# Four edits to the order of work around the layer norms of a two-layer graph network

## The chip, the cores and the metric

One core of one Trainium2 chip runs the whole program. The metric is device time in microseconds (us) of one execution, from the inputs in HBM to the output in HBM. Several executions are timed; their median counts.

## The reference

x is 128 graphs of 128 nodes with 256 features, adj a 0/1 matrix per graph. All is float32.

```python
h = maximum(layernorm(x), 0)
x = x + L0(h, adj)       # scores = leaky_relu(h W a1 + (h W a2)^T), masked by adj, softmax; elu(attn @ h)
h = maximum(layernorm(x), 0)
x = x + L1(h, adj)       # three attention blocks:
# for l in 0..2:
#   scores = si + sj^T + attn_b[l], leaky 0.2, mask = adj + eye, softmax
#   agg = attn @ x ;  h = layernorm(x + agg) * g1 + beta1
#   ff  = gelu(h @ W1[l] + b1[l]) @ W2[l] + b2[l]
#   x   = layernorm(h + ff) * g2 + beta2
```

W1 is 256 x 1024, W2 1024 x 256. Every matmul of the feed-forward part is made of three: each operand is split into a high part that the fast format holds and a low part that is the rest, and high x high, high x low and low x high are added.

## The kernel before

**Units, groups, steps.** Four graphs are a group (32 groups), and a group in one of the three blocks of L1 is a unit (96 units, run in chunks of 8 groups: 8 units of layer 0, 8 of layer 1, 8 of layer 2, then the next chunk). Every engine runs the same list of steps, `body`, from step -6 to step 97. Step s does the feed-forward part of unit s on PE (`hidden(0..7)`: eight blocks of 128 hidden features; `second(0..3)`: the four graphs), and beside it, on the other engines, the norm ahead of it for unit s + 1, the softmax for unit s + 2, the dots for unit s + 3 and the norm behind it for unit s - 1. Steps 24 to 47 are a loop that is run twice; 72 to 97 are written out.

**Stages of L0.** Each group passes through L0 in four stages, one step after another: early (norm of the input, dots, mask), middle (scores, exponentials), late (aggregation, ELU, residual), end (norm of the result). The first eight groups do so from step -6 on, one in every step. From step 2 on a group starts in every third step. So from step 5 to 73 three kinds of step take turns:
- an **opening step** (5, 8, 11, ... 71) has the early stage of one group and the end stage of another,
- a **mask step** (6, 9, ...) has a middle stage,
- an **ELU step** (7, 10, ...) has a late stage.

Three in this order are called a triple here. Step 74 has the last end stage; steps 75 to 94 have no stage of L0: **bare steps**. Steps 0 to 4 still end one of the first eight groups each and run another order of DVE's work.

**Engines.** PE multiplies. ACT evaluates: for each hidden block the Gelu twice (L872 writes the high half g_hi, L874 the exact value back into the PSUM bank), exponentials (L739), the products of the norms (L746, L801), and `turned` (L843), which copies the turned exponentials into et. DVE makes the low halves (`g_low(c)`, L1000: exact value minus high half), the sums and statistics, the shifts of the norms (L990) and the dots (L969, `row_dots`). POOL makes the inverse roots (L1310, `inverse_root`), products and additions of rows (`by_graph`, L374) and the masks (L1374, L1365). SP issues the DMAs. Each engine works through its own list in order; counted semaphores tie them.

**PE in a step** (L687 on): hidden(0), the scores of unit s + 2 (`next_scores`, L556), which wait for the dots of that unit and for et_ready, since et is read out of the same bank; the aggregates of unit s + 1 (L569), which read et; hidden(1) to hidden(7); the turned rows; second(0) to second(3). hidden(1) writes into a bank that DVE must have emptied first (`v_done`, L1207: vb, the first graph pair). second(0) reads low half c before its block c.

**DVE in a step, from 5 on** (L1245 to L1280): vb, half 0, the sums of the rows of unit s + 1, half 1, its variance, the lows, half 2, its norm, half 3, the statistics of the input (early stage), halves 4 and 5, the statistics of vb (`second_statistics`), half 6, the variance of vb (`second_variance`), half 7, the variance of the input, the low rows, the shifts of both, then

```python
next_dots(range(T // 2))
made_variance(); next_inverses(); made_shift()
if not only_middle(s): first_lows()
next_dots(range(T // 2, T))
elu_sums(); first_inverses(); first_dots(); next_heads(); first_heads()
```

next_dots are the eight dots of unit s + 3, first_dots the eight of the early stage's group; made_variance and made_shift belong to the end stage, and POOL's root (`made_root`) lies between the two. ACT's `make_rows` (L746) waits for made_shift, and `turned` stands behind make_rows in ACT's list.

**POOL in a step**: root of the norm of unit s + 1, the rows hb (eight instructions), the root of unit s - 1, the roots of the stages, the masks, residual_sum (late stage), weight halves in the first chunk (L1326), then, behind a wait for all dots of the step, `affine` of unit s - 1: xo times g2, plus beta2; for a unit of the last layer `residual` adds the kept rows xin[1] besides. The twelve instructions of that are L374 too. ACT writes xo before (L746), and SP stores it after.

**The start.** DVE awaits the constants aw_in at the beginning of step -3. In step -1 ACT runs: exponentials, make_rows, ELUs, first exponentials, turned.

## Time and profile before

| | us |
|---|---|
| runs shown | 2748.73, 2750.09, 2750.27 |
| median | 2750.09 |
| the profiled execution | 2747.82 |
| its span | 2746.0 |
| PE busy | 2657.8 |
| ACT busy | 2200.4 |
| DVE busy | 2136.6 |
| POOL busy | 1676.9 |

The span runs from the first to the last instruction; 1.8 us of the profiled execution lie around it. PE's mean granted clock is 0.988 of 2.4 GHz: it is at half speed, 1.2 GHz, in parts of the first 128 us only. A matmul is pipelined, so PE's gaps between one matmul's modelled end and the next one's start tell more than its busy share. A releaser ("<-") is what ended an idle time; where an engine waits for several semaphores the last one is named.

### The profile page before, as it was taken

How to read it: one execution, taken by the hardware profiler on the slowest of the kernel's cores; microseconds unless marked ns; L12 is line 12 of the kernel's file. 1: busy time of each engine (PE TensorE's matmuls, PEld its weight loads, DVE VectorE, ACT ScalarE, POOL GpSimd, SP SyncE). 2: the span in 40 equal slices, each digit the busy share in tenths (PEclk: the TensorE clock that was granted, in tenths of full speed). 3: DMA queues.
4: the chain of work that ended last, by engine and by line, in shares of the span. 5: the costliest groups of instructions: out<-in, count | busy, mean ns of one | idle time of the engine just before them, and what ended most of it. 6: DMA issues, size and time to landing. Idle time of an engine off the chain costs nothing.

```text
span 2746.0 us, 53334 instructions
## 1 busy us (share of the span) xinstructions
PE 2657.8 (97%) x16772; PEld 2394.5 (87%) x16868; DVE 2136.6 (78%) x7999; ACT 2200.4 (80%) x4494; POOL 1676.9 (61%) x2181
## 2 busy tenths in 40 slices
PE   5799999999999999999999999999999999999997
PEld 4689888988888888988888989898888898998997
DVE  7998788877787877787877787877788767677674
ACT  5899888888788888887888888888888777777774
POOL 4567657656666656566666566556676554454555
PEclk7899999999999999999999999999999999999999
DMA  6222222222222222112322121222132211111121
GB/s 217 79 70 72 92 73 88 67 77 87 81 76 69 75 67 71 62 64 82 100 82 80 50 77 66 78 66 80 62 103 82 68 36 53 47 41 53 51 64 54
DMA packets 118589, 203.43 MB, mean 74 GB/s; under 512 B 12800, under 2 KB 85536, under 8 KB 118304
## 3 DMA queue, kind: packets, MB, share of 16 engines
q1 hardware_dynamic: 118304, 199.97, 22.4%
q8 instruction: 137, 2.24, 0.3%
q14 instruction: 148, 1.21, 0.1%
HBM read 116.05 MB, written 83.89 MB: 73 GB/s over the span
## 4 chain that ended last, share of the span: by engine, by line
PE 72%; DVE 11%; POOL 8%; issue 5%; ACT 3%; DMA 0%; SPq 0%; DVEq 0%; POOLq 0%; ACTq 0%
PE bank L610 32%; PE bank L593 27%; PE ps_u L569 7%; POOL xo L374 3%; DVE g_lo L1000 3%; DVE st L974 2%; PE ps_u L651 2%; POOL rs L1310 2%; POOL hb L374 2%; PE ps_s L564 2%; DVE ub L1093 2%; PE ps_s L556 2%; DVE ub L969 1%; ACT g_hi L872 1%; ACT bank L874 1%
## 5 line engine op out<-in xcount | busy, mean ns | idle before, releaser
L610 PE MATMUL bank<-w_hi,g_hi 128*128 128x256 f32 x3072 | 892.0, 290 | 15.4 <-DVE g_lo L1000 15.2
L610 PE MATMUL bank<-w_hi,g_lo 128*128 128x256 f32 x3072 | 866.8, 282 | 0.0
L610 PE MATMUL bank<-w_lo,g_hi 128*128 128x256 f32 x3072 | 865.6, 282 | 0.0
L872 ACT ACTIVATE g_hi<-bank,b_eff 128x512 fp32r<-128x512 f32 x768 | 529.3, 689 | 334.0 <-PE bank L593 327.3
L1000 DVE TENSOR_TENSOR g_lo<-bank,g_hi 128x512 fp32r<-128x512 f32 x768 | 519.0, 686 | 202.6 <-ACT bank L874 187.9
L593 PE MATMUL bank<-zt_hi,w_hi 128*128 128x512 f32 x1536 | 633.2, 412 | 9.1 <-DVE g_lo L1000 5.5
L593 PE MATMUL bank<-zt_hi,w_lo 128*128 128x512 f32 x1536 | 608.3, 396 | 0.0
L593 PE MATMUL bank<-zt_lo,w_hi 128*128 128x512 f32 x1536 | 607.1, 395 | 0.0
L610 PEld LDWEIGHTS bank<-w_hi,g_hi 128*128 128x128 f32 x3072 | 579.9, 189 | 24.1 <-DVE g_lo L1000 23.1
L610 PEld LDWEIGHTS bank<-w_lo,g_hi 128*128 128x128 f32 x3072 | 580.2, 189 | 0.7
L610 PEld LDWEIGHTS bank<-w_hi,g_lo 128*128 128x128 f32 x3072 | 579.6, 189 | 0.0
L1310 POOL TENSOR_TENSOR rs<-ve,neg_half 128x4 f32<-128x4 f32 x256 | 266.6, 1041 | 445.6 <-DVE ve L985 441.0
L874 ACT ACTIVATE bank<-bank,b_eff 128x512 f32<-128x512 f32 x768 | 508.4, 662 | 25.0
L374 POOL TENSOR_TENSOR xo<-xo,g_row 128x256 f32<-128x256 f32 x380 | 268.8, 739 | 201.4 <-ACT xo L746 136.5
L374 POOL TENSOR_TENSOR hb<-ub,g_row 128x256 f32<-128x256 f32 x384 | 272.4, 741 | 173.3 <-DVE ub L1093 168.2
L593 PEld LDWEIGHTS bank<-zt_hi,w_hi 128*128 128x128 f32 x1536 | 290.1, 189 | 75.7 <-DVE g_lo L1000 10.8
L593 PEld LDWEIGHTS bank<-zt_hi,w_lo 128*128 128x128 f32 x1536 | 289.6, 189 | 67.6
L593 PEld LDWEIGHTS bank<-zt_lo,w_hi 128*128 128x128 f32 x1536 | 290.4, 189 | 60.0
L1207 DVE TENSOR_TENSOR vb<-bank,hb 128x512 f32<-128x512 f32 x192 | 129.9, 688 | 242.9 <-PE bank L610 214.6
L374 POOL TENSOR_TENSOR hb<-hb,bb_row 128x256 f32<-128x256 f32 x384 | 277.8, 756 | 7.5
L969 DVE CUSTOM_DVE_ANT_0 ub<-xb,aw_row 128x256 f32<-128x256 f32 x744 | 280.5, 432 | 1.6 <-issue 0.5
L374 POOL TENSOR_TENSOR xo<-xo,beta_row 128x256 f32<-128x256 f32 x380 | 267.5, 736 | 7.5
(96 smaller groups left out, 4146.1 us busy)
## 6 DMA issues: line engine op xcount, KB each, us to landing
xb<-x_scratch SPq DMA_DIRECT2D x88, 512.0 KB, 4.0
x_scratch<-xo SPq DMA_DIRECT2D x64, 512.0 KB, 4.8
xin<-in_x SPq DMA_DIRECT2D x38, 512.0 KB, 4.8
r_scratch<-elu_r SPq DMA_DIRECT2D x32, 512.0 KB, 3.0
xin<-r_scratch SPq DMA_DIRECT2D x32, 512.0 KB, 4.5
out<-xo SPq DMA_DIRECT2D x32, 512.0 KB, 3.4
m<-m_scratch SPq DMA_DIRECT2D x96, 128.0 KB, 3.9
x_scratch<-h SPq DMA_DIRECT2D x24, 512.0 KB, 2.9
```

What stands on the lines that cost most here:

```text
L374: ins = eng.tensor_tensor(dst[:, t, :], src[:, t, :], other(t), op)
L556: pe.matmul(scores[:, t * P:(t + 1) * P], dot[:, 1, t:t + 1].to_broadcast((P, P)), ident[:, :], is_transpose=True, start=(t == 0), stop=Tr ...
L564: mm = pe.transpose(dst[:, t * P:(t + 1) * P], e[:, t, :], ident[:, :])
L569: pe.matmul(sums[t // 2][:, t % 2 * D:(t % 2 + 1) * D], weights[:, t, :], rows[:, t, :], start=True, stop=True).then_inc(done, 1)
L593: mm = pe.matmul(bank[turn[c]][:, :], w[:, l, k, c * P:(c + 1) * P], z[:, k, :], start=(n == 0), stop=(n == 3 * K1 - 1))
L610: mm = pe.matmul(y, g[:, c, r * P:(r + 1) * P], w[:, l, c, :], start=(c == 0 and n == 0), stop=(c == C - 1 and n == 2))
L872: act.activation(g_hi[:, c, :], block_in, ACT.Gelu, bias=bias).then_inc(g_hi_ready, 1)
L874: act.activation(block_in, block_in, ACT.Gelu, bias=bias).then_inc(gelu_done, 1)
L969: dve.tensor_tensor_reduce(junk[:, j, :], rows[:, t, :], vec(j), 1.0, 0.0, ALU.mult, ALU.add, dot[:, j, t:t + 1]).then_inc(ready, 1)
L1000: dve.tensor_tensor(g_lo[:, c, :], bank[turn[c]][:, :], g_hi[:, c, :].bitcast(F32), ALU.subtract).then_inc(g_lo_ready, 1)
L1207: dve.tensor_tensor(vb[:, 2 * r:2 * r + 2, :], ps_y[r].rearrange("p (t d) -> p t d", d=D), hb[(s - 1) % 2][:, 2 * r:2 * r + 2, :], ALU.add ...
L1310: pool.tensor_tensor(rs[:, :], ve[:, :], neg_half[:, :], ALU.pow).then_inc(rs_ready, 1)
```

## The change

- DVE, steps 5 on: halves 4 to 7 follow each other; the statistics of vb come behind them, then a copy of four columns into `spare` (it stands between statistics and variance, whose wait it takes), then the variance.
- DVE, where a step has an early and an end stage (the opening steps): the order behind made_variance is next_inverses, the first four dots of the early group, made_shift, the last four next_dots, the last four first_dots. first_dots from step 0 on write their products into the other half of the scratch ub and await `h_scaled` and `zt_ps` instead of all next dots.
- POOL, units of the last layer: `residual` adds beta2 onto the kept rows xin[1] in place. It stands behind the masks and ahead of residual_sum, behind a wait for the first four next dots. affine then multiplies xo by g2 and adds xin[1]: eight instructions behind ACT's xo instead of twelve. For the last unit DVE's affine does the same, and the addition onto xin[1] is POOL's.
- ACT, step -1: turned comes ahead of the ELUs and the first exponentials.
- DVE, start: the wait for the constants moves from the beginning of step -3 to just ahead of its next_dots.

```diff
--- before.py
+++ after.py
@@ -254,7 +254,7 @@
         nm2_ready = sem("nm2_ready")
         z2_ready = sem("z2_ready")
         xo_scaled = sem("xo_scaled")
-        xo_shifted = sem("xo_shifted")
+        r_shifted = sem("r_shifted")
         xo_ready = sem("xo_ready")
 
 
@@ -382,14 +382,15 @@
             eng.wait_ge(z2_ready, st.nth(u))
             by_graph(eng, xo, xo, lambda t: g2_row[:, l, :], ALU.mult).then_inc(xo_scaled, 1)
             eng.wait_ge(xo_scaled, st.nth(u))
-            by_graph(eng, xo, xo, lambda t: beta2_row[:, l, :], ALU.add).then_inc(xo_shifted if last else xo_ready, 1)
+            if last:
+                eng.wait_ge(r_shifted, st.nth0(group(u)))
+            by_graph(eng, xo, xo, lambda t: xin[1][:, t, :] if last else beta2_row[:, l, :], ALU.add).then_inc(xo_ready, 1)
 
         def residual(eng, st, u):
 
             if layer(u) == L - 1:
-                eng.wait_ge(xo_shifted, st.nth0(group(u)))
                 eng.wait_ge(r_in, 16 * st.nth0(group(u)))
-                by_graph(eng, xo, xo, lambda t: xin[1][:, t, :], ALU.add).then_inc(xo_ready, 1)
+                by_graph(eng, xin[1], xin[1], lambda t: beta2_row[:, L - 1, :], ALU.add).then_inc(r_shifted, 1)
 
         block = ctx.enter_context(nc.Block())
 
@@ -855,10 +856,14 @@
                     high_rows()
                     if s == -1:
                         next_exps()
+                        make_rows()
+                        turned()
+                        elus()
+                        first_exps()
+                        return
                     make_rows()
                     elus()
-                    if s < -1:
-                        next_exps()
+                    next_exps()
                     first_exps()
                     turned()
                     return
@@ -1034,9 +1039,11 @@
                     if v0 is not None:
                         if s >= 0:
                             dve.wait_ge(h0_ready, st.nth0(v0, T))
-                        if live(s + 3) and s >= 0:
-                            dve.wait_ge(dots_ready, st.nth(s + 3, 2 * T))
-                        row_dots(st.nth0, v0, dots0, h0[v0 % 2], lambda j: v_row[:, j, :], dots0_ready, junk,
+                            if live(s + 1):
+                                dve.wait_ge(h_scaled, st.nth(s + 1))
+                                dve.wait_ge(zt_ps, st.nth(s + 1))
+                        row_dots(st.nth0, v0, dots0, h0[v0 % 2], lambda j: v_row[:, j, :], dots0_ready,
+                                 vb if s < 0 else ub[:, 2:4, :],
                                  graphs, made=h0_ready if s < 0 else None)
 
                 def sum_rows():
@@ -1185,6 +1192,8 @@
                     made_shift()
                     first_dots(range(T // 2, T))
                     low_rows()
+                    if s == -3:
+                        dve.wait_ge(aw_in, 16 * 2)
                     next_dots(range(T))
                     first_heads()
                     next_heads()
@@ -1253,10 +1262,11 @@
                 input_statistics()
                 g_low(4)
                 g_low(5)
+                g_low(6)
+                g_low(7)
                 second_statistics()
-                g_low(6)
+                dve.tensor_copy(spare[:, 2:2 + T], neg_half[:, :])
                 second_variance()
-                g_low(7)
                 input_variance()
                 if v1 is not None and early_step(v1) >= 0:
                     mask_sums(v1)
@@ -1269,22 +1279,27 @@
                 next_dots(range(T // 2))
                 made_variance()
                 next_inverses()
-                made_shift()
-                if not only_middle(s):
-                    first_lows()
-                next_dots(range(T // 2, T))
-                elu_sums()
-                first_inverses()
-                first_dots()
+                if v0 is not None and v3 is not None:
+                    first_dots(range(T // 2))
+                    made_shift()
+                    next_dots(range(T // 2, T))
+                    first_dots(range(T // 2, T))
+                else:
+                    made_shift()
+                    if not only_middle(s):
+                        first_lows()
+                    next_dots(range(T // 2, T))
+                    elu_sums()
+                    first_inverses()
+                    first_dots()
                 next_heads()
                 first_heads()
                 if late_piece(s) is not None:
                     late_low_half(*late_piece(s))
                 if s - 2 == U - 1:
                     affine(dve, st, s - 2)
-                    residual(dve, st, s - 2)
-
-            steps(dve, body, {-3: lambda: dve.wait_ge(aw_in, 16 * 2), -1: rows})
+
+            steps(dve, body, {-1: rows})
 
 
         @block.gpsimd
@@ -1410,6 +1425,10 @@
                     made_root()
                 mask()
                 first_mask()
+                if live(s - 1) and layer(s - 1) == L - 1:
+                    if live(s + 3):
+                        pool.wait_ge(dots_ready, st.nth(s + 3, 2 * T, T))
+                    residual(pool, st, s - 1)
                 residual_sum()
                 if late_piece(s) is not None:
                     late_low_half(*late_piece(s))
@@ -1420,7 +1439,6 @@
                     if v0 is not None:
                         pool.wait_ge(dots0_ready, st.nth0(v0, 2 * T))
                     affine(pool, st, s - 1)
-                    residual(pool, st, s - 1)
 
             steps(pool, body, {})
```

## Rows read from the trace of the kernel before

**Rows 1.** The page, part 1: busy us, share of the span, instructions of each engine.

```profile
PE 2657.8 (97%) x16772; PEld 2394.5 (87%) x16868; DVE 2136.6 (78%) x7999; ACT 2200.4 (80%) x4494; POOL 1676.9 (61%) x2181
```

**Rows 2.** Waits of PE: line, releaser; us in total, times, longest.

```profile
PE bank L610 <- DVE g_lo L1000: 15.2, 29, 1.4
...
PE bank L593 <- issue: 1.6, 1, 1.6
```

**Rows 3.** Sums by stretch: us, busy us (instructions) by engine, PEclk, DMA share, GB/s.

```profile
2472.35:2524.86 52.51, 52.41 (x339) 47.56 (x339) 37.54 (x132) 39.01 (x74) 26.55 (x37) 1.00 0.15 46
...
913.76:940.74 26.98, 26.45 (x170) 23.86 (x170) 23.06 (x90) 22.52 (x45) 17.45 (x22) 1.00 0.29 94
...
940.74:996.08 55.34, 55.23 (x356) 50.10 (x357) 42.35 (x160) 45.88 (x96) 32.20 (x43) 1.00 0.16 56
...
sum 752.66, PE 739.58 PEld 665.03 DVE 593.85 ACT 616.13 POOL 512.94; mean PE 246.53 PEld 221.68 DVE 197.95 ACT 205.38 POOL 170.98
```

**Rows 4.** Timeline of DVE, step 29: start us, us, line, operation, [idle before <-releaser].

```profile
927.90 1.40 DVE L974 BATCH_NORM_STATS2 st<-vb 128x6 f32<-128x256 f32 x4
...
930.58 0.68 DVE L1000 TENSOR_TENSOR g_lo<-bank,g_hi 128x512 fp32r<-128x512 f32 x1
...
933.11 0.43 DVE L969 CUSTOM_DVE_ANT_0 ub<-xb,aw_row 128x256 f32<-128x256 f32 x1
...
934.50 1.40 DVE L974 BATCH_NORM_STATS2 st<-elu_r 128x6 f32<-128x256 f32 x4
...
936.42 0.17 DVE L985 TENSOR_SCALAR ve<-mv 128x4 f32<-128x4 f32 x1
...
937.71 0.16 DVE L990 SCALAR_TENSOR_TENSOR nm<-mv,rs 128x4 f32<-128x4 f32 x1 [1.04 <-POOL rs L1310]
...
938.20 0.82 DVE L969 CUSTOM_DVE_ANT_0 ub<-xb,aw_row 128x256 f32<-128x256 f32 x1
...
938.96 0.41 DVE L969 CUSTOM_DVE_ANT_0 ub<-xb,aw_row 128x256 f32<-128x256 f32 x1
```

**Rows 5.** Timeline of PE, end of step 29 and start of step 30.

```profile
931.31 0.39 PE L610 MATMUL bank<-w_hi,g_hi 128*128 128x256 f32 x1 [0.47 <-DVE g_lo L1000]
...
942.14 0.60 PE L556 MATMUL ps_s<-ident,dots 128*128 128x128 f32 x4
...
944.33 0.58 PE L593 MATMUL bank<-zt_hi,w_hi 128*128 128x512 f32 x1
```

**Rows 6.** Timeline of ACT, step 29.

```profile
928.24 0.66 ACT L874 ACTIVATE bank<-bank,b_eff 128x512 f32<-128x512 f32 x1
...
939.90 0.57 ACT L843 ACTIVATE et<-ps_s 128x512 f32<-128x512 f32 x1
```

**Rows 7.** Timeline of DVE, step 21, a mask step of layer 2.

```profile
703.31 1.38 DVE L1093 TENSOR_SCALAR ub<-ub,mv,rs 128x256 f32<-128x256 f32 x4 [1.52 <-POOL rs L1310]
```

**Rows 8.** Timeline of POOL, step 29.

```profile
930.74 2.09 POOL L1310 TENSOR_TENSOR rs<-ve,neg_half 128x4 f32<-128x4 f32 x2
...
937.91 2.17 POOL L1374 TENSOR_SCALAR m<-adj_i 128x512 bf16<-128x512 int32 x1
```

**Rows 9.** Timelines of PE, ACT and DVE, steps -3 to 0.

```profile
97.11 1.08 PE L556 MATMUL ps_s<-ident,dots 128*128 128x128 f32 x4 [3.43 <-ACT et L843]
...
96.30 0.67 ACT L843 ACTIVATE et<-ps_s 128x512 f32<-128x512 f32 x1
...
104.11 0.69 DVE L1000 TENSOR_TENSOR g_lo<-bank,g_hi 128x512 fp32r<-128x512 f32 x1 [0.54 <-ACT bank L874]
...
39.27 1.41 DVE L974 BATCH_NORM_STATS2 st<-ub 128x6 f32<-128x256 f32 x4 [4.21 <-DMA ab_col<-in_L_gnn_attn_b]
...
41.07 13.65 PE L546 MATMUL bank<-beta_col,raw 128*128 128x1 f32 x64
```

**Rows 10.** Timelines of DVE, step 11, and PE, step 12.

```profile
441.99 0.95 DVE L969 CUSTOM_DVE_ANT_0 ub<-h,v_row 128x256 f32<-128x256 f32 x1
...
447.50 0.50 PE L593 MATMUL bank<-zt_hi,w_hi 128*128 128x512 f32 x1 [0.88 <-DVE vb L1207]
```

## The prediction

> **What bounds the kernel now.** I read the page first, for who is busy: PE for 97% of the span [rows 1]. Next the waits of PE, for what the rest is: beside the first steps, small waits on DVE's low halves, 15.2 us in 29 places [rows 2]. Then the sums by stretch, for the steps they sit in [rows 3]. Two bare steps take 52.51 us, 26.26 each; a mask step with the ELU step behind it takes 55.34, without a gap. So a triple without stalls is 26.26 + 55.34 = 81.60 us. In layers 0 and 1 the opening step is 26.98, 0.72 over the bare one, and that is all such a triple loses. The nine triples that hold the last-layer units (three stretches of three, from 581, 1243 and 1907 us) take 752.66 us: 18.3 above 9 x 81.60, of which 1.6 is PE's own stop where the loop turns [rows 2]. They lose 16.7 us.
>
> The timelines say where. In opening step 29 DVE has half 5 behind it at 927.90, does vb's statistics first (to 929.30), then half 6 and vb's variance, and starts half 7 at 930.58 [rows 4]; PE sits 0.47 us for it [rows 5]. ACT had its input ready at 928.24 + 0.66 = 928.90 [rows 6]. In layer 2 POOL stands in twelve products and additions when the next norm's root is due: DVE waits 1.52 us for it in step 21 [rows 7], and PE behind DVE.
>
> **Low halves in one row.** Half 6 would run at 927.90, half 7 when ACT is done, 928.94 to 929.63. PE needs it at about 930.84 (0.47 before 931.31), so the opening step falls to the bare 26.26: **-0.72**, and PE reaches its next step 0.72 earlier. vb's statistics then end near 930.95 and its variance 0.7 later (as 935.90 to 936.59, the copy included) [rows 4]. POOL's two roots of 2.09 us run from 931.72 to 933.81, against 930.74 to 932.83 [rows 8], and the dots behind the shifts begin at 934.09 instead of 933.11 [rows 4]. In steps of the other kinds the statistics move behind a half that DVE must await, and the low rows come some 1.5 us later. The cover there is PE's work: by the same count the ELU step's aggregates, the nearest taker, keep about 1 us in hand. Without it every ELU step would pay.
>
> **Dots around the root.** From the first dot to the made group's variance is 936.59 - 933.11 = 3.48, so the variance ends at 937.57. Four dots of the new input follow in 1.39 (933.11 to 934.50) [rows 4], and the made group's shift starts at 938.96 instead of 937.71. The 1.04 us of waiting is gone, but what was waited for comes later. POOL begins its mask 937.91 - 936.59 = 1.32 after that variance, at 938.89, 0.07 before the shift. A DVE instruction that came 0.29 us after the mask's start took 0.82 instead of 0.42 [rows 4, 8]. The bounds for the shift are no delay and that 0.40, its end 939.12 or 939.52; I take the second, the nearest row.
>
> ACT goes from that shift to the end of et in 940.47 - 937.87 = 2.60 us [rows 4, 6], and PE's next scores wait for et: where that is seen they start 0.14 us behind its end [rows 9]. So they run at 942.26 (or 941.86). PE would be ready at 942.14 - 0.72 = 941.42 [rows 5]. **New wait: 0.84 (or 0.44)**, ahead of the scores of the mask step. A triple of layer 0 or 1 comes to -0.72 + 0.84 = +0.12 (or -0.28); eleven of them, opened by steps 14 to 62: **+1.3 (or -3.1)**. The dots' new waits on scaled and turned rows hide: the first half of the next dots has awaited both. Their other scratch costs nothing; operands and sizes stay.
>
> **Residual rows in place.** POOL's work stays at twelve products and additions per last-layer unit, but four leave the path behind the norm, so the next root is no longer late: the stall of [rows 7] goes, and the opening step's with it. The four now follow the mask. In an opening step that ends at 938.89 + 2.17 = 941.06 [rows 8]; the residual rows are long there, since SP issues their load right behind the previous unit's store. DVE is then at its last four dots, from 939.52 + 1.39 = 940.91. The nearest row is step 11, where four POOL additions met such dots: 0.95 each instead of 0.42, so 0.88 apart instead of 0.35 [rows 10]. That gives 940.91 + 0.35 + 3 x 0.88 = 943.90; two short heads, which meet POOL's last additions, about 0.8 with them; vb's first half, 0.69, ends near 945.4. In step 12 PE started right behind such a half [rows 10]. PE's second hidden block would want it at 944.33 - 0.72 = 943.61 [rows 5]: **1.8, taken as 1.9, lost in the mask step**, the 0.84 included. Bounds: 0.84 (POOL hits nothing) and 2.3 (both heads hit in full). Eight triples lose 1.9, and the one at the loop's turn, whose 1.6 us covers most, 0.4: 15.6 against 16.7, **-1.1**. In ELU steps the same meeting falls into DVE's own wait for the ELU parts, in mask steps ahead of its wait for PE.
>
> The rule that speaks most against this is in the Trainium skill, SBUF — State Buffer, section "SBUF: two separate sides": the port pair that VectorE and GpSimd share is an exclusive lock, held for a whole instruction. Taken literally it gives the first rival below; here a mask of 2.17 us cost DVE 0.40 [rows 4, 8], so the sum goes by the rows.
>
> **The rest.** Steps 5, 8 and 11 end in weight halves, and vb is already what PE waits for behind them. DVE's stalls there change from 1.04 to 0.35 (half 7), about 0.55 (shifts) and 0.08 (copy): **-0.2** for the three. In step -1 et no longer stands behind ELU and exponentials; PE's scores now wait 3.43 us for it. They would then wait for dots that end at about 94.9, and DVE, dense through step 0, gains its stall of 0.54 at 104.11 [rows 9] and some 0.15 ahead of it: **-0.7** (0 to -2.2). The constants' wait frees 4.21 us of DVE before 39.27, but PE stands in the bias products from 41.07 for 13.65 us either way [rows 9]: **0**. At the end unit 94 leaves POOL some 0.6 earlier, while unit 95's residual now awaits its load on POOL and meets DVE's product: **0** (-0.6 to +0.6).
>
> **Sum:** +1.3 - 1.1 - 0.2 - 0.7 + 0 = -0.7 us. The profiled execution took 2747.82, 2.27 below the median; on the median of 2750.09 that is **2749.4 us**. About 0.2%, 5.5 us, is what a measurement of this kernel can tell. The forecast's own bounds (unmet mask -4.4, heavier heads +3.2, start and end) give 2742 to 2755.
>
> **Rivals.** First, the shift waits for POOL's whole mask. Then it ends at 941.06 + 0.16 = 941.22, the scores run at 943.96, 2.54 late: eleven triples lose 1.82 net, 20.0, and the last-layer ones, with dots and vb also 1.7 later, 3.6 each, 14 more than now; with the rest +33, **2783**. For it: the new shift falls just behind the mask's start. Against it: a dot 1.05 us into a mask took 0.41 [rows 4]. This is the lock of the Trainium skill's page named above; by that rule it would be the result. Chance 0.04. The same in part: the path from et to the scores costs 20 x 0.1 = 2 us for every 0.1 us that the shift ends behind 939.52, and from 0.3 us on (939.8) the change is slower: chance 0.10, around **2757**.
>
> Second, POOL's residual additions don't slow the dots, or the heads absorb it. Then the last-layer triples lose 0.84 each, the loop's none: 6.7 - 16.7 = -10.0, in all **2740**; with the mask unmet too, 3.5 - 16.7 = -13.2 and -3.1, **2733**. For it: a POOL instruction slowed only what came soon behind its start [rows 4]. Against it: step 11, where every dot was hit [rows 10]. Chance 0.27 together, 0.09 of it for the second.
>
> Third, the opening stall is ACT's and not DVE's order: no half comes earlier, et is not exposed, and the time stays within the forecast's range. Half 7's input at 928.90 against its start at 930.58 [rows 4, 6] leaves it 0.02.
>
> **The numbers.** Forecast 0.57; with the third rival no change has 0.59; faster 0.27; slower 0.04 + 0.10 = 0.14. The range leaves out the far rivals of both sides (0.09 and some 0.08): 2738 to 2757.
>
> **What would show it.** Right: opening steps of 26.3 without a wait on low halves; a wait of 0.4 to 0.8 us of PE's scores on ACT's et in some twenty mask steps; in layer 2 dots of 0.95 and a PE wait on vb, and no DVE wait on POOL's root. Wrong: triples of layer 2 near 82.4 us (POOL harmless), or mask steps over 28 in layers 0 and 1 (the shift held by the mask).

## The result, and the profile after

The changed kernel takes 2735.68 us (median of 5 runs, 2735.10 to 2736.28) against 2750.27 for the kernel before on the same chip: ratio 0.9949, interval 0.9938 to 0.9960. It is faster by 14.6 us; no change had been forecast, and the result lies 2.3 us below the range. Its profiled execution has a span of 2734.1 us against 2746.0, so 11.9 us of the gain can be followed in the two traces.

The page, part 1, after [rows 1]:

```profile
PE 2653.5 (97%) x16772; PEld 2385.7 (87%) x16868; DVE 2193.9 (80%) x8088; ACT 2203.1 (81%) x4494; POOL 1703.4 (62%) x2185
```

PE does the same work and is busy 4 us less; DVE is busy 57 us longer and the kernel is faster. The waits of PE after [rows 2]:

```profile
PE bank L594 <- DVE vb L1216: 4.9, 12, 1.8
PE bank L611 <- DVE g_lo L1005: 4.6, 6, 1.4
PE ps_s L557 <- ACT et L844: 4.2, 16, 0.4
PE bank L594 <- issue: 1.6, 1, 1.6
```

The 29 waits for low halves are down to 6, all in the first steps; waits for et (16) and for vb (12) have come instead. The sums by stretch after [rows 3]: two bare steps, opening step 29, the two steps behind it, and the sum of the nine layer-2 triples:

```profile
2460.10:2512.61 52.51, 52.41 (x339) 47.53 (x340) 38.31 (x134) 39.24 (x74) 26.61 (x37) 1.00 0.15 46
907.62:933.88 26.26, 26.21 (x171) 23.79 (x170) 22.74 (x89) 20.61 (x41) 16.47 (x22) 1.00 0.31 96
933.88:989.63 55.75, 55.39 (x355) 49.95 (x356) 43.21 (x164) 47.79 (x100) 33.33 (x44) 1.00 0.16 56
...
sum 746.44, PE 738.25 PEld 661.76 DVE 631.80 ACT 616.07 POOL 529.18; mean PE 246.08 PEld 220.59 DVE 210.60 ACT 205.36 POOL 176.39
```

The opening step has the length of a bare one, the mask step has 0.42 more than before, and the nine layer-2 triples have become 6.2 us shorter.

**Opening step 29 after** [rows 4, 6, 8], timelines of DVE, ACT, POOL and of PE in step 30:

```profile
931.15 0.17 DVE L990 TENSOR_SCALAR ve<-mv 128x4 f32<-128x4 f32 x1
...
931.38 0.43 DVE L974 CUSTOM_DVE_ANT_0 ub<-h,v_row 128x256 f32<-128x256 f32 x1
...
932.77 0.16 DVE L995 SCALAR_TENSOR_TENSOR nm<-mv,rs 128x4 f32<-128x4 f32 x1
...
933.20 0.82 DVE L974 CUSTOM_DVE_ANT_0 ub<-xb,aw_row 128x256 f32<-128x256 f32 x1
```

```profile
934.95 0.58 ACT L844 ACTIVATE et<-ps_s 128x512 f32<-128x512 f32 x1
```

```profile
931.40 1.28 POOL L1325 TENSOR_TENSOR rs<-ve,neg_half 128x4 f32<-128x4 f32 x1 [3.83 <-DVE ve L990]
932.65 0.25 POOL L1320 TENSOR_TENSOR spare<-neg_half 128x1 f32<-128x1 f32 x1
932.97 2.11 POOL L1389 TENSOR_SCALAR m<-adj_i 128x512 bf16<-128x512 int32 x1
```

```profile
935.67 0.62 PE L557 MATMUL ps_s<-ident,dots 128*128 128x128 f32 x4 [0.26 <-ACT et L844]
```

POOL's root takes 1.28 us beside DVE's dots, not the 1.01 it took while DVE stood still, so the mask starts 0.20 behind the shift's start. The root before:

```profile
936.67 1.01 POOL L1310 TENSOR_TENSOR rs<-ve,neg_half 128x4 f32<-128x4 f32 x1 [3.84 <-DVE ve L985]
```

The mask slows one of the last next dots instead (0.82). From the end of the shift to the end of et are 2.60 us, as forecast.

**Opening step 20, layer 2, after**, timelines of DVE, POOL and of PE in step 21:

```profile
684.05 0.17 DVE L990 TENSOR_SCALAR ve<-mv 128x4 f32<-128x4 f32 x1
...
687.46 0.41 DVE L974 CUSTOM_DVE_ANT_0 ub<-h,v_row 128x256 f32<-128x256 f32 x1
...
688.15 0.94 DVE L974 CUSTOM_DVE_ANT_0 ub<-h,v_row 128x256 f32<-128x256 f32 x1
...
689.02 0.93 DVE L974 CUSTOM_DVE_ANT_0 ub<-h,v_row 128x256 f32<-128x256 f32 x1
...
689.88 0.68 DVE L1086 TENSOR_SCALAR si<-dots,ab_col 128x4 f32<-128x4 f32 x1
...
690.55 1.28 DVE L1216 TENSOR_TENSOR vb<-bank,hb 128x512 f32<-128x512 f32 x2
```

```profile
687.96 3.26 POOL L374 TENSOR_TENSOR xin<-xin,beta_row 128x256 f32<-128x256 f32 x4
```

```profile
691.28 0.50 PE L594 MATMUL bank<-zt_hi,w_hi 128*128 128x512 f32 x1 [0.23 <-DVE vb L1216]
```

POOL's additions start half a microsecond behind the last four dots, not 0.15 as worked out. The first two dots escape, two take 0.93 or 0.94 and one head 0.68 instead of the 0.22 that it takes in step 29. vb's first half follows and PE waits for it.

### The profile page after: what moved, and what is told of

Its sections match the earlier page's. It is cut to its first block, busy times and chain, and to the rows that moved or that the text cites. A ratio compares the mean times of both kernels' runs of the same rounds, so it can differ in the third digit from the quotient of the medians.

```text
span 2734.1 us, 53457 instructions
## 1 busy us (share of the span) xinstructions
PE 2653.5 (97%) x16772; PEld 2385.7 (87%) x16868; DVE 2193.9 (80%) x8088; ACT 2203.1 (81%) x4494; POOL 1703.4 (62%) x2185
## 4 chain that ended last, share of the span: by engine, by line
PE 74%; DVE 12%; POOL 6%; ACT 5%; issue 4%; DMA 0%; DVEq 0%; SPq 0%; POOLq 0%; ACTq 0%
PE bank L594 31%; PE bank L611 30%; PE ps_u L570 7%; POOL hb L374 3%; DVE ub L974 3%; PE ps_u L652 2%; DVE st L979 2%; POOL rs L1325 2%; PE ps_s L557 2%; PE ps_s L565 2%; ACT g_hi L877 1%; ACT bank L879 1%; DVE g_lo L1005 1%; DVE ub L1100 1%; ACT h L747 1%
## 5 line engine op out<-in xcount | busy, mean ns | idle before, releaser
L1325 POOL TENSOR_TENSOR rs<-ve,neg_half 128x4 f32<-128x4 f32 x256 | 275.7, 1080 | 554.4 <-DVE ve L990 553.0
L974 DVE CUSTOM_DVE_ANT_0 ub<-xb,aw_row 128x256 f32<-128x256 f32 x744 | 311.2, 475 | 1.4
L374 POOL TENSOR_TENSOR hb<-hb,bb_row 128x256 f32<-128x256 f32 x384 | 272.3, 741 | 7.5
L747 ACT ACTIVATE xo<-vb,nm,rs 128x256 f32<-128x256 f32 x384 | 199.4, 595 | 28.6 <-DVE nm L995 19.7
```

Of the source, the lines that this page charges most:

```text
L374: ins = eng.tensor_tensor(dst[:, t, :], src[:, t, :], other(t), op)
L747: a = act.activation(dst[:, t, :], src[:, t, :], function, bias=nm[:, t:t + 1], scale=rs[:, t:t + 1])
L974: dve.tensor_tensor_reduce(junk[:, j, :], rows[:, t, :], vec(j), 1.0, 0.0, ALU.mult, ALU.add, dot[:, j, t:t + 1]).then_inc(ready, 1)
L1325: pool.tensor_tensor(rs[:, :], ve[:, :], neg_half[:, :], ALU.pow).then_inc(rs_ready, 1)
```

## The experiments

The change has five edits; the table holds all kernels that were timed: medians, and lengths of single steps taken from PE's first hidden matmul to the next step's. Steps 29 and 30 are an opening and a mask step of layers 0 and 1, 44 and 45 of layer 2; 48 follows the loop's turn, 95 runs to the end of the span. "5 at" is when step 5 starts. y1, which is the kernel before profiled once more, stands in the text alone.

| kernel | median | 5 at | 29 | 30 | 44 | 45 | 48 | 95 |
|---|---|---|---|---|---|---|---|---|
| before | 2750.3 | 249.28 | 26.98 | 26.90 | 27.31 | 27.88 | 27.55 | 38.08 |
| changed | 2735.7 | 248.37 | 26.26 | 27.32 | 26.27 | 27.96 | 29.25 | 38.44 |
| x1 rows | 2764.1 | 251.76 | 26.26 | 27.67 | 26.28 | 29.50 | 29.29 | 40.34 |
| x2 dots | 2741.7 | 250.49 | 27.19 | 26.97 | 27.32 | 26.88 | 26.98 | 38.03 |
| x3 residual | 2750.8 | 251.58 | 26.99 | 26.90 | 27.01 | 28.17 | 29.63 | 36.29 |
| x4 constants | 2747.3 | 247.28 | 26.98 | 26.90 | 27.33 | 27.94 | 27.48 | 38.12 |
| y2 et, step -1 | 2750.2 | 250.78 | 26.97 | 26.90 | 27.30 | 27.90 | 27.53 | 38.05 |
| y3 rows, dots | 2743.3 | 251.57 | 26.26 | 27.31 | 26.27 | 28.29 | 28.83 | 40.28 |
| x5 changed, no residual edit | 2740.0 | 249.50 | 26.26 | 27.31 | 26.28 | 28.27 | 28.61 | 40.26 |
| x6 changed, dots as before | 2773.7 | 248.97 | 26.26 | 27.65 | 26.27 | 31.22 | 31.19 | 38.27 |
| z1 changed, no additions | 2728.7 | 249.38 | 26.26 | 27.32 | 26.27 | 27.31 | 28.79 | 35.97 |
| x7 changed, et first | 2731.0 | 247.71 | 26.26 | 26.88 | 26.27 | 27.97 | 30.62 | 38.14 |
| x8 = x5, et first | 2735.9 | 251.15 | 26.26 | 26.88 | 26.27 | 28.28 | 28.74 | 40.27 |
| y4 = x7, residual in the gap | 2727.1 | 248.48 | 26.26 | 26.88 | 26.27 | 27.54 | 29.19 | 38.11 |
| z2 = y4, next dots first | 2726.8 | 248.11 | 26.26 | 26.88 | 26.27 | 27.54 | 28.75 | 38.35 |

### One edit at a time, on the kernel before

**x1**, halves 4 to 7 in one row, alone:

```diff
                 g_low(5)
-                second_statistics()
                 g_low(6)
-                second_variance()
                 g_low(7)
+                second_statistics()
+                dve.tensor_copy(spare[:, 2:2 + T], neg_half[:, :])
+                second_variance()
                 input_variance()
```

> The kernel before with one edit alone: halves 4 to 7 in one row, the statistics and variance of vb behind them. Theory: the wait on a low half goes from the opening steps (26.98 to 26.27 in layers 0 and 1), DVE's shift comes about 1.0 us later, et with it, and PE's scores in the mask step wait at most 0.2 us for et; the late root of layer 2 stays. About 0.5 us per triple, 10 us in all: 2740. Rival 1 (the stall is ACT's and not the order of DVE's list): no change, 2750. Rival 2 (the later variance and shift are paid in the ELU steps and by et): slower or equal, 2750 to 2755.

Measured: 2764.08 us, ratio 1.0051 (1.0037 to 1.0064), slower than any theory had it. The opening step does fall to 26.26. But the rest of DVE's list is then a microsecond late and PE is 0.72 early: vb is late in every mask step, and in layer 2 the root is later still. DVE in step 45, and two waits of PE:

```profile
1377.42 1.38 DVE L1093 TENSOR_SCALAR ub<-ub,mv,rs 128x256 f32<-128x256 f32 x4 [1.54 <-POOL rs L1311]
```

```profile
PE bank L593 <- DVE vb L1207: 14.6, 23, 2.3
PE bank L593 <- DVE g_lo L1000: 12.0, 8, 1.6
```

**x2**, the split dots, alone (their other scratch and waits, which belong to it, are not printed here):

```diff
-                made_shift()
-                if not only_middle(s):
-                    first_lows()
-                next_dots(range(T // 2, T))
-                elu_sums()
-                first_inverses()
-                first_dots()
+                if v0 is not None and v3 is not None:
+                    first_dots(range(T // 2))
+                    made_shift()
+                    next_dots(range(T // 2, T))
+                    first_dots(range(T // 2, T))
+                else:
...
```

> The kernel before with one edit alone: the dots of the opening step split around the shift of the made rows. Theory: DVE's wait of 1.04 us for POOL's root goes, the shift comes 0.5 us later than before, but PE is not earlier either, so et is not awaited (1.67 us were in hand), and nothing PE waits for comes earlier: no change, 2749 to 2750, less 1 us at most in the steps 5 to 12. Rival (the split by itself is worth something, because vb is ready earlier): a microsecond per triple, 2730 to 2740. Rival on the other side: the later et is awaited by the scores: 2755.

Measured: 2741.68 us, ratio 0.9971 (0.9960 to 0.9981). The theory of no gain falls, and with it a step of the prediction: layer-2 mask steps come down to 26.88, with no stall at all. POOL's products of the xo rows stand behind a wait for all dots of the step. With DVE's 1.04 us of waiting gone, and a short gap ahead of the new input's dots with it, the products start 27.79 us into step 20 instead of 29.17, and the next root is in time although POOL still has twelve instructions there. POOL's first products, before (step 20 starts at 664.51) and in x2 (661.85), then DVE in step 21, where [rows 7] had 1.52 us of waiting:

```profile
693.68 2.79 POOL L374 TENSOR_TENSOR xo<-xo,g_row 128x256 f32<-128x256 f32 x4 [2.79 <-issue]
```

```profile
689.64 2.79 POOL L374 TENSOR_TENSOR xo<-xo,g_row 128x256 f32<-128x256 f32 x4 [1.17 <-issue]
```

```profile
698.44 0.68 DVE L1000 TENSOR_TENSOR g_lo<-bank,g_hi 128x512 fp32r<-128x512 f32 x1
699.26 1.38 DVE L1095 TENSOR_SCALAR ub<-ub,mv,rs 128x256 f32<-128x256 f32 x4
```

By PE's steps the nine layer-2 triples gain 7.4 us and steps 5 to 13 2.9, while the triples of layers 0 and 1 lose 1.8, for a reason that was not looked for.

**x3**, the residual rows in place, alone:

```diff
                 first_mask()
+                if live(s - 1) and layer(s - 1) == L - 1:
+                    if live(s + 3):
+                        pool.wait_ge(dots_ready, st.nth(s + 3, 2 * T, T))
+                    residual(pool, st, s - 1)
                 residual_sum()
...
                     affine(pool, st, s - 1)
-                    residual(pool, st, s - 1)
```

> The kernel before with one edit alone: beta2 added onto the kept rows behind the masks, eight instead of twelve POOL instructions behind the dots. Theory: in the nine layer-2 triples the late root goes, opening steps return to 26.98 and mask steps to 27 or a little over; the additions slow the dots they meet by 0.2 to 0.3 us each, which PE doesn't see: about 1.0 us per triple, 2739 to 2742. Rival (the prediction's step: each addition that meets a dot costs DVE 0.53 us, and vb is late for PE): mask steps stay near 27.8, 2747 to 2750.

Measured: 2750.83 us, ratio 1.0002 (0.9993 to 1.0011): nearest to the rival, the prediction's own step. The late root goes (44 is 0.3 shorter), and vb becomes late by as much and a little more (45 is 0.3 longer):

```profile
PE bank L594 <- DVE vb L1208: 11.7, 12, 2.2
```

**x4**, the wait for the constants just ahead of the dots that need them, alone:

```diff
                     low_rows()
+                    if s == -3:
+                        dve.wait_ge(aw_in, 16 * 2)
                     next_dots(range(T))
...
-            steps(dve, body, {-3: lambda: dve.wait_ge(aw_in, 16 * 2), -1: rows})
+            steps(dve, body, {-1: rows})
```

> The kernel before with one edit alone: DVE awaits the constants just ahead of the dots of step -3. Theory from the changed kernel's trace: PE's 64 bias products behind it take 10.5 instead of 13.7 us since TensorE's granted clock is up for part of them (0.64 against 0.50 in that stretch), and step 0 starts about 2.3 us earlier; 2748, or 2749.5 if a dip of the clock in step 2 (1.4 us there) comes with it. Rival (the prediction's step: PE stands in the bias products for 13.65 us either way): no change of step 0's start, 2750.

Measured: 2747.33 us, ratio 0.9991 (0.9982 to 1.0000). Step 0 starts at 87.60 us instead of 90.92. The bias products of PE in x4 [rows 9], then the stretch from 40 to 56 us of x4 and of the kernel before:

```profile
40.04 10.68 PE L546 MATMUL bank<-beta_col,raw 128*128 128x1 f32 x64
```

```profile
40.00:56.00 16.00, 15.78 (x92) 15.40 (x92) 14.93 (x70) 12.33 (x35) 9.19 (x8) 0.68 1.04 382
```

```profile
40.00:56.00 16.00, 16.00 (x74) 15.73 (x74) 15.22 (x70) 9.88 (x27) 8.03 (x8) 0.50 0.97 363
```

The same 64 products take 10.68 us instead of 13.65, and the granted clock is not at 1.2 GHz for the whole of them. But it is not the edit that shortens them. In x1, x2, x3, y2 and y3, which keep the old wait, they take 10.55 to 10.73 us, and step 0 still starts at 90.8 to 91.4. In x8, which has the edit, they take 13.65 at a granted clock of 0.50, and step 0 starts at 90.66. The products in y2, then in x8:

```profile
39.97 10.68 PE L546 MATMUL bank<-beta_col,raw 128*128 128x1 f32 x64
```

```profile
41.01 13.65 PE L546 MATMUL bank<-beta_col,raw 128*128 128x1 f32 x64
```

What the edit moves is DVE's list: its last statistics of an input ahead of step 0 start at 72.80 us in x4 and at 76.12 before, and step 0 follows 14.80 behind in both. In x8 DVE loses the gain again. It stops for 2.41 us ahead of an instruction on PE's scores. The profile names no releaser, but the scores stand behind the long products and start at 55.41 us (51.47 in x4):

```profile
58.12 0.29 DVE L959 CUSTOM_DVE_ANT_0 ps_s<-ps_s,e 128x128 f32<-128x128 f32 x1 [2.41 <-issue]
```

So the edit is worth its 3 us where the products are short. What makes them short in one profile and long in another, the runs do not show.

**y2**, et ahead of the ELUs in step -1, alone:

```diff
                         next_exps()
+                        make_rows()
+                        turned()
+                        elus()
+                        first_exps()
+                        return
...
```

> The kernel before with one edit alone: in step -1 ACT copies et ahead of the ELUs and the first exponentials. Theory from the changed kernel's trace: the wait of 3.4 us for et in step 0 turns into two of 1.1, but step 0 stays at 37 us, because the granted clock is down for longer in it: 2749 to 2751. Rival (the prediction's term): the wait is replaced by one for dots and 0.7 us are gained, up to 2.2: 2748.

Measured: 2750.21 us, ratio 1.0003 (0.9994 to 1.0012): no gain, as the theory had it. Step 0 takes 36.96 us against 37.02, though the one wait has become two smaller ones. The granted clock is 0.91 in it against 0.92, so the theory's reason is borne out in small part only.

**y1**, the kernel before once more.

> The kernel before once more, for a second profile of its start. Theory: the step 2 of the profile shown of before (32.27 us, granted clock 1.00 in 178 to 184 us) was the odd one, since four kernels that leave that step alone had 33.7 to 33.8 with the clock near 0.7 behind the same wait; this profile has 33.7 there and nothing else changed. Rival (the edits at the start cause the fall of the clock in step 2): 32.3 again.

Measured: step 2 takes 32.32 us again; the theory that the first profile was the odd one falls. Every other kernel here has 33.6 to 35.0 in that step, those too that leave it alone, like y2. The waits in it are the same; the granted clock behind them is not. First the changed kernel, then the one before:

```profile
176.23:182.00 5.77, 4.85 (x26) 4.65 (x27) 5.70 (x24) 4.86 (x19) 3.65 (x5) 0.70 0.16 47
```

```profile
178.22:184.00 5.78, 4.87 (x35) 4.56 (x36) 5.71 (x25) 4.89 (x19) 3.66 (x5) 1.00 0.17 50
```

Why the clock falls behind that wait in one and not in the other stays open; it is worth 1.4 us. The profile of before and y1 are alone in this, and together with x8 alone in having the long bias products.

**y3**, halves in a row and split dots together: the two hunks of x1 and x2.

> The kernel before with two edits: halves in one row and split dots. Theory: alone they gave +13.7 and -8.7; together the microsecond that the split saves DVE pays for the row, opening steps are 26.27, mask steps of layers 0 and 1 27.3 (et), of layer 2 28.1 to 28.3 (root), the last step 40.2: 2742 to 2744, hardly different from the split dots alone. Rival (they add up): 2755.

Measured: 2743.26 us, ratio 0.9977 (0.9967 to 0.9987): not the sum of +13.7 and -8.7. The microsecond that the split saves DVE is the one that the row costs the list behind it. All five edits timed alone come to +3.3 us (+13.7, -8.7, +0.5, -3.1 and +0.9), together to -14.6.

### One edit undone, on the changed kernel

**x5**: POOL's residual rows as before, the x3 hunk undone.

> The changed kernel with one edit undone: POOL adds beta2 and the kept rows behind the dots as before (twelve instructions there). Theory: the late root of layer 2 was paid for by the wait for all dots, and the split dots alone let POOL start a microsecond earlier; without the additions on the last four dots vb comes 1.5 us earlier and the root about 0.1 us late, so layer-2 mask steps fall from 27.8 to 27.3 and the step at the loop's turn by 1.5: 2729 to 2732. Rival (the prediction's step: taking four instructions off the path is what removes the late root): mask steps of layer 2 at 28 or more with a wait on low halves, 2740.

Measured: 2740.00 us, ratio 0.9964 (0.9950 to 0.9977): the rival. Without the additions vb is in time, but the root is late again, by half of what it was. DVE in step 21:

```profile
700.11 1.38 DVE L1099 TENSOR_SCALAR ub<-ub,mv,rs 128x256 f32<-128x256 f32 x4 [0.83 <-POOL rs L1325]
```

So in the changed kernel the residual edit is worth about 4 us: about 0.3 in each layer-2 mask step and 1.8 in step 95, less 0.6 in step 48.

**x6**: the dots in the old order, the x2 hunk undone.

> The changed kernel with one edit undone: the dots of the opening step in the order of before, with DVE's wait for POOL's root ahead of them. Theory: the halves in one row put DVE's list 1.0 us later, which only the split dots give back; mask steps wait for vb in every triple, most in layer 2 (28.5), and two or three of them lose more when TensorE's granted clock falls behind the wait: 2750 to 2762. Rival (the edits add up: 2735.7 plus the 8.7 that the split dots gained alone): 2744.

Measured: 2773.67 us, ratio 1.0088 (1.0075 to 1.0102), worse than the theory's range. Without the split the other edits cost 24 us. PE's waits for vb, and the middle of step 21:

```profile
PE bank L594 <- DVE vb L1214: 31.9, 23, 2.8
```

```profile
698.88:705.30 6.42, 3.90 (x21) 2.96 (x20) 6.28 (x24) 4.53 (x9) 4.88 (x7) 0.97 0.30 102
705.30:712.00 6.70, 6.70 (x25) 5.44 (x26) 6.33 (x26) 3.99 (x8) 5.86 (x8) 0.77 0.35 122
712.00:729.90 17.90, 17.90 (x133) 16.81 (x131) 15.46 (x53) 16.02 (x38) 13.30 (x17) 1.00 0.18 58
```

A wait of 2.46 us ends at 705.29; behind it the granted clock is 0.77 over 6.7 us, at 1.2 GHz in part of them. The wait costs more than itself: the step takes 31.01, 1.65 more than 26.90 and the wait, where step 9, with the clock at 1.00 behind 1.84 us, takes 0.6 more.

**z1**: POOL's additions left out, with one element per partition in their place.

```diff
-                by_graph(eng, xin[1], xin[1], lambda t: beta2_row[:, L - 1, :], ALU.add).then_inc(r_shifted, 1)
+                eng.tensor_tensor(xin[1][:, 0, 0:1], xin[1][:, 0, 0:1], beta2_row[:, L - 1, 0:1], ALU.add).then_inc(r_shifted, 1)
```

> The changed kernel without POOL's additions onto the kept rows: one element per partition is added in their place, so beta2 of the last layer is left out of all other elements. Theory: what the last layer's mask steps lose over those of layers 0 and 1 is the additions meeting two of the four last dots and a head; without them vb is in time and the root early, mask steps of layer 2 fall from 27.8 to 27.3 (et alone), nine times 0.5, the loop's turn by 1.5 more: 2730. Rival (vb is late by the order of DVE's list, whatever POOL does): they stay at 27.8, 2735.

Measured: 2728.65 us, ratio 0.9921 (0.9906 to 0.9937), the theory. Layer-2 mask steps come to 27.31, what those of layers 0 and 1 have, and PE's waits for vb shrink to those of steps 6, 9, 12 and 48:

```profile
PE bank L594 <- DVE vb L1216: 2.5, 4, 1.4
```

### Towards a faster kernel

**x7**: in opening steps ACT copies et ahead of the made rows; **x8**: the same on x5.

```diff
                 second_norm()
+                if v3 is not None:
+                    turned()
+                    make_rows()
+                    return
                 make_rows()
```

> The changed kernel with one more edit: in the opening steps ACT copies et ahead of the made rows instead of behind them, so that et no longer hangs on the shift. Theory: PE's wait of 0.25 us for et before the scores and the longer scores step go (mask steps of layers 0 and 1 from 27.32 to 26.90), layer 2 keeps its wait for vb: eleven times 0.42, 2731. Rival (the turned scores are not in the bank yet at that place, so that ACT waits there and its second norm or made rows come late): 2736 or slower.

> Both: et ahead of the made rows, and the residual rows behind the dots as in the kernel before. Theory: every triple comes near its floor of 81.60 us, since neither et nor vb nor the root is late; twenty mask steps at 26.90: 2722 to 2726. Rival (with et out of the way the root is the next thing late in layer 2): layer-2 mask steps at 27.3 with a wait on low halves, 2727 to 2730.

Measured: 2731.00 us for x7, ratio 0.9932 (0.9918 to 0.9945), the theory to the microsecond: step 30 is 26.88. That it fits so well is partly luck. The triples of layers 0 and 1 gain 5.0 us and not 4.6, and step 48 loses 1.4: behind a wait of 1.82 us for vb its granted clock is 0.94, where the changed kernel has 1.00 behind one of 1.83. In the other mask steps of layer 2 the wait for vb takes all of the gain (8.6 us of PE's waits instead of 4.9). x8 is 2735.94, ratio 0.9947 (0.9934 to 0.9961): neither expectation; the late root keeps step 45 at 28.28.

**y4**: x7, with POOL's additions in the 3.74 us in which POOL stands idle ahead of its root of the made rows; **z2**: y4 with the last next dots ahead of the shift.

```diff
-                if v3 is not None and v3 >= CH:
+                opening = v3 is not None and v3 >= CH
+                if opening:
+                    kept_rows()
                     made_root()
                 mask()
                 first_mask()
-                if live(s - 1) and layer(s - 1) == L - 1:
...
+                if not opening:
+                    kept_rows()
                 residual_sum()
```

`kept_rows` holds the lines taken out. z2, against y4:

```diff
-                    first_dots(range(T // 2))
-                    made_shift()
                     next_dots(range(T // 2, T))
-                    first_dots(range(T // 2, T))
+                    made_shift()
+                    first_dots()
```

> The changed kernel with et ahead of the made rows, and in the opening steps POOL's four additions of the residual rows ahead of its root of the made rows, in the 3.7 us in which it stands idle there, behind the first four dots, instead of behind the masks. Theory: the additions meet DVE's statistics and only the first one or two of the following dots, the root comes up to 0.9 us later, DVE waits 0.6 us for it, and the last eight dots run at their own pace: vb comes 0.6 us earlier, the wait of 0.5 to 0.7 us in the layer-2 mask steps goes, the loop's turn loses 0.7 less: 2725 to 2727. Rival (the additions slow the statistics as much as the dots, or the root delays the last dots by as much): 2731 or slower.

> The kernel with et ahead of the made rows and the residual rows in POOL's gap (2727.1), with one more edit: the last four next dots go ahead of the shift, all eight dots of the new input behind it. Theory: its layer-2 mask steps lose 0.45 to 0.65 because the scores wait for the next dots, and here these end 1.5 us earlier, while the rest of DVE's list is as long as before: mask steps of layer 2 at 26.9 to 27.1, 2723 to 2725. Rival (the dots hit by POOL's additions are then the next dots again, and vb is late in their place): 2727.

Measured: 2727.09 us for y4, ratio 0.9922 (0.9909 to 0.9936), the theory. POOL in step 20:

```profile
681.58 2.81 POOL L374 TENSOR_TENSOR xin<-xin,beta_row 128x256 f32<-128x256 f32 x4 [1.73 <-DVE dots L978]
684.35 1.20 POOL L1329 TENSOR_TENSOR rs<-ve,neg_half 128x4 f32<-128x4 f32 x1
```

DVE beside them:

```profile
681.42 1.40 DVE L983 BATCH_NORM_STATS2 st<-elu_r 128x6 f32<-128x256 f32 x4
...
683.73 0.94 DVE L978 CUSTOM_DVE_ANT_0 ub<-h,v_row 128x256 f32<-128x256 f32 x1
```

The four additions run mostly beside DVE's statistics, in 2.81 us instead of 3.26, and the root starts right behind them. One dot meets the last of them (0.94), where two and a head were hit before. z2 is 2726.83, ratio 0.9918 (0.9904 to 0.9931): the rival; step 45 stays at 27.54. One dot still meets the additions (0.94) and one the mask (0.82), vb comes no earlier in its step, and PE waits for it instead of the scores' dots. Both are faster than the kernel before and the changed one, whose ratio was 0.9949.

## Why the prediction was wrong

No change was forecast, and the spans of the two profiles differ by 11.9 us. Three terms carry most of it: the mask steps of layer 2, where 1.9 us were taken and 1.0 measured; the bound taken for the shift, 0.84 where 0.42 was measured; and the constants' wait, which was put at nothing.

| term of the sum | forecast | by PE's steps |
|---|---|---|
| before step 0 (the constants' wait) | 0 | -2.3 |
| steps 0 to 4 (et in step -1) | -0.7 | +1.4 |
| steps 5 to 13 | -0.2 | -2.2 |
| eleven triples, layers 0 and 1 | +1.3, bound -3.1 | -2.9 |
| nine triples, layer 2 | -1.1 | -6.2 |
| the end | 0 | +0.3 |
| sum | -0.7 | -11.9 |

**Halves in a row: right.** Every opening step is bare, but for the loop's turn in step 47; step 29 is 0.72 shorter, and ELU steps stay at 28.43. In x1 DVE's order alone does it, which rules out the third rival, an opening stall that is ACT's.

**"I take the second, the nearest row": failed, and the other bound held.** The shift was taken to meet the mask's start (0.40 late). POOL's root grew to 1.28 beside the four dots that the change puts there, the mask came 0.20 behind the shift, and the mask steps lose 0.42, not 0.84. That turns +1.3 into -2.9, near the bound of an unmet mask. The wait itself is seen: 16 times, 0.26 us each on average.

**"1.8, taken as 1.9, lost in the mask step": mis-sized.** The nine triples lose 746.44 - 9 x 81.60 = 12.0 us; without the loop's 1.6 and the 2.4 of step 48, that is 8.0 for the other eight, 1.0 each. The mechanism is the one named: z1 takes the additions away and 0.6 of the 1.0 goes; the rest is et. The size was off because the additions began 0.50 behind the dots, not 0.15, so two dots were hit and not three, and because nothing delayed the shift: vb's first half ends 7.2 us behind the made variance's start, not 8.0. The triples came to 82.5 to 82.7, near the 82.4 that was to tell of harmless additions, although the additions do hit.

**"One at the loop's turn ... 0.4": wrong the other way.** Step 48 has lost 2.4. DVE turns the loop too, with 2.91 us of waiting for nothing that the profile shows, and vb stands behind that. The changed kernel, then z1:

```profile
1434.26 1.29 DVE L1216 TENSOR_TENSOR vb<-bank,hb 128x512 f32<-128x512 f32 x2 [2.91 <-issue]
```

```profile
1431.92 0.69 DVE L1216 TENSOR_TENSOR vb<-bank,hb 128x512 f32<-128x512 f32 x1 [4.20 <-issue]
```

POOL's additions are the smaller part of it. Without them DVE's list ends 1.7 us earlier against PE's step, but the stop is 4.20 us, and step 48 still takes 28.79. It takes 26.98 with the split dots alone (x2), 28.83 with the row as well (y3) and 29.29 with the row alone (x1): most of the loss comes with the row. Why the stop's length differs stays open.

**"What was waited for comes later": the value of the split was missed.** The prediction counted the split dots by the shift alone. It saw that POOL's twelve instructions make the root late, and gave the cure to the residual edit. But the twelve start when all dots are done, and the split lets them start 1.4 us earlier: alone it removes the stall of [rows 7] and 8.7 us (x2), and without it the rest of the change is slower than before by 24 us (x6). In the sum this error hid, since the stall goes when both edits are in; with the row and the split but without the residual edit, 0.83 of its 1.52 us are left (x5).

**"The constants' wait ... 0": failed.** The sum held step 0 to PE's bias products, 13.65 us "either way". They take that in both profiles of before and in x8, where the edit indeed gains nothing, but 10.5 to 10.8 in all other profiles. There DVE's list sets the start of step 0, and the edit moves it by 3.3 us (x4). How much of the -2.3 would be seen in the timed runs is not shown.

**"-0.7" in step -1: failed.** The et move gave nothing (y2). Of the +1.4, step 2 has all: the granted clock falls in it, as in every profile but the two of before, and no run ties that to an edit (y1).

**"-0.2 for the three" steps 5, 8 and 11: mis-sized.** These pairs of an opening and a mask step fell by 0.35, 0.60 and 1.22. x1 and x2 show why no single stall could be priced there: the row alone makes steps 9 and 12 3.1 us longer, with a fall of the granted clock in both, the split alone 0.8 and 1.2 shorter.

**The rivals.** The mask did not hold the shift. Rival two was nearest in its time (2733 with the mask unmet), but not in its reason: POOL's additions do slow the dots. The lock rule of the Trainium skill (SBUF — State Buffer, section "SBUF: two separate sides") does not fit here as a whole: beside a mask of 2.10 or 2.11 us one dot took 0.82 or 0.83, and the two behind it 0.41 each while the mask still ran. In neither step was a dot held for the whole of the mask.

**What stays open.** 2.7 of the 14.6 us lie outside the two profiled executions: before's lay 2.45 us (y1 0.9) below the median of the runs beside it, the changed kernel's did not. The short step 2 of both profiles of before would explain half of that if timed runs mostly lack it; that was not shown. What sets the granted clock in the first 100 us and in step 2 is open too.

## What to carry to other kernels

A wait that is removed is to be followed to everything that stands behind the engine's list, not only to what it was waiting for: here the gain was another engine's start. Edits that move the same list by a microsecond in opposite directions do not add up; price them together, or take them out one at a time on both kernels. A difference that hangs on the granted clock belongs to an edit only if the kernels without that edit don't show it. Before putting work on an engine's critical side, look for the stretch in which that engine idles and its neighbour runs something that it does not disturb.

## What the runs showed of the hardware

- A POOL addition of 128x256 slows a DVE dot of the same shape from 0.41 to 0.94 us, and even an instruction on 128x4 from 0.22 to 0.68; the additions themselves go from 2.81 to 3.26 for four. Beside DVE's batch statistics (1.40 with and without, y4) the four take 2.81.
- The granted clock falls behind some waits of PE and not behind others of the same length: in x6 step 6 has a wait of 1.85 us, a granted clock of 0.94 and 30.80 us, step 9 a wait of 1.84, a clock of 1.00 and 29.35 us.
- The turn of the loop stops DVE for 2.9 to 4.2 us and PE for 1.4 to 2.0, over all profiles.
